# Attention scores from two fp32r parts instead of three bf16 parts, in a four-batch cross-attention block on one Trainium2 core

## What is computed

```python
B, LQ, LK, D, H, HD, INNER = 4, 256, 512, 256, 16, 16, 1024
# layer 0
q = layer_norm(x, ln1_w, ln1_b) @ q_w + q_b        # per head of 16
k = ctx @ k_w + k_b;  v = ctx @ v_w + v_b
scores = where(mask, q k^T / sqrt(16), lowest)
out = softmax(scores) v
hidden = out @ cproj_w + cproj_b + x
x = hidden + gelu(layer_norm(hidden, ln2_w, ln2_b) @ fc_w + fc_b) @ proj_w + proj_b
# layer 1, one head, on the same context
scores = (x w_q^T) (ctx w_k^T)^T / 16
x = x + alpha * (softmax(scores) (ctx w_v^T)) w_o^T
```

## Time and profile before

| | |
|---|---|
| Median of three runs | 315.48 us |
| Lowest, highest | 314.37, 318.81 us |
| Span of the profiled execution, first to last instruction | 310.4 us |
| Its own time | not given apart; the median is 5.1 us above the span |
| Busy: PE, weight loads, DVE, ACT, POOL | 87%, 63%, 67%, 61%, 38% |
| Mean granted TensorE clock | 0.960 |
| DMA | 21163 packets, 21.62 MB |

### The profile page before, as it was taken

One profiled execution on the slowest core, in us unless ns is written; L12 is line 12 of the kernel. 1 busy time (PEld: TensorE's weight loads), 2 busy tenths in 40 slices (PEclk: granted clock), 3 DMA queues, 4 the chain that ended last, 5 costly groups with the idle time before them and its releaser, 6 DMA issues.

```text
span 310.4 us, 5591 instructions
## 1 busy us (share of the span) xinstructions
PE 268.6 (87%) x2073; PEld 195.3 (63%) x2073; DVE 206.8 (67%) x367; ACT 187.8 (61%) x351; POOL 118.3 (38%) x174
## 2 busy tenths in 40 slices
PE   3974769998788999899979997999998989898995
PEld 2670236683266676665866766665966777677974
DVE  5774777729657859576569598657388655366854
ACT  1553367759464686967454887766466678426622
POOL 3574652523111369830012688430131256324100
PEclk9997599989797999999999999999999999999999
DMA  5597552522254002124112112121130000000001
GB/s 176 173 155 104 141 157 94 163 72 67 78 154 126 12 25 67 57 74 126 64 38 99 28 59 70 34 80 51 34 130 3 0 1 2 2 0 0 2 34 36
DMA packets 21163, 21.62 MB, mean 70 GB/s; under 512 B 4608, under 2 KB 17616, under 8 KB 21136
## 3 DMA queue, kind: packets, MB, share of 16 engines
q1 hardware_dynamic: 16880, 13.09, 14.8%
q0 software_dynamic: 1648, 3.87, 4.9%
q10 hardware_dynamic: 2608, 4.30, 4.6%
HBM read 10.50 MB, written 1.05 MB: 37 GB/s over the span
## 4 chain that ended last, share of the span: by engine, by line
PE 56%; ACT 13%; POOL 11%; DVE 9%; issue 5%; DMA 3%; ACTq 2%; POOLq 0%; DVEq 0%
PE work_ps L602 10%; PE om L679 8%; PE s L652 7%; PE work_ps L589 6%; PE s L669 6%; PE work_ps L606 5%; DVE neg_max L1442 4%; ACT q_stack L1100 3%; ACT probs L1109 2%; POOL y_l L1833 2%; PE s L602 2%; DMA q_stack<-qp 2%; POOL kf L1793 1%; ACT fx L1136 1%; POOL ft L1828 1%
## 5 line engine op out<-in xcount | busy, mean ns | idle before, releaser
L1442 DVE TENSOR_REDUCE neg_max<-s 128x1 f32<-128x512 f32 x128 | 83.5, 683 | 23.1 <-PE s L652 21.9
L1109 ACT ACTIVATE probs<-s 128x512 f32<-128x512 f32 x128 | 75.3, 601 | 32.4 <-PE s L669 31.8
L652 PE MATMUL s<-k_stack,q_stack 97*128 97x512 bf16 x128 | 49.8, 424 | 8.2 <-DMA q_stack<-qp 4.9
L669 PE MATMUL s<-q_stack,k_stack 109*128 109x256 bf16 x256 | 51.8, 286 | 2.0 <-ACT probs L1109 1.0
L679 PE MATMUL om<-probs,vals 128*17 128x256 f32 x512 | 34.5, 390 | 0.2 <-ACT probs L1109 0.2
L669 PEld LDWEIGHTS s<-q_stack,k_stack 109*128 109x128 bf16 x256 | 21.0, 102 | 19.0 <-ACT probs L1109 5.0
L652 PEld LDWEIGHTS s<-k_stack,q_stack 97*128 97x128 bf16 x128 | 13.0, 102 | 28.8 <-DVE neg_max L1442 14.3
L1763 POOL CAST max_cols<-neg_max 128x8 bf16<-128x8 f32 x16 | 6.1, 381 | 63.2 <-DVE neg_max L1442 63.2
L1100 ACT ACTIVATE q_stack<-om 13x1024 bf16<-13x1024 bf16 x16 | 16.3, 1017 | 9.1 <-PE om L659 8.8
L679 PEld LDWEIGHTS om<-probs,vals 128*17 128x17 f32 x512 | 12.0, 98 | 13.7 <-issue 6.2
L1123 ACT ACTIVATE y_h<-work_ps 128x512 fp32r<-128x512 f32 x12 | 7.2, 596 | 16.3 <-PE work_ps L606 14.5
(11 more groups left out here) (328 smaller groups left out, 724.5 us busy)
## 6 DMA issues: line engine op xcount, KB each, us to landing
k_stack<-kp SPq DMA_DIRECT2D x96, 64.0 KB
q_stack<-qp SPq DMA_DIRECT2D x81, 32.0 KB
cx<-in_ctx_dram SPq DMA_DIRECT2D x4, 512.0 KB, 4.7
pcx<-in_ctx_dram ACTq DMA_DIRECT2D x3, 512.0 KB, 3.6
xz<-in_x_dram SPq DMA_DIRECT2D x4, 256.0 KB, 2.7
raw_late<-in_L_xattn_fc_w_dram POOLq DMA_DIRECT2D x1, 1024.0 KB, 5.4
raw_late<-in_L_xattn_proj_w_dram POOLq DMA_DIRECT2D x1, 1024.0 KB, 6.7
h<-in_x_dram ACTq DMA_DIRECT2D x3, 256.0 KB, 2.6
```

The costliest lines, as they stand in the source:

```text
L652: pe.matmul(s1[:, s1_bank(b, SLOTS * g + s), :], q_stack[0:ROW_MAX, hd, chunk(t)], k_stack[0:ROW_MAX, hd, :], start=True, stop=True).then_ ...
L669: mm = pe.matmul(s2[:, s2_bank(b, SLOTS * g + s), i * LQ:(i + 1) * LQ], k_stack[:, hd, chunk(k)], q_stack[:, hd, :], start=True, stop=True)
L1109: act.activation(probs[:, g % 2, s // 2, k:k + 2, :], s2[:, s2_bank(b, SLOTS * g + s), :].rearrange("p (k n) -> p k n", k=2), ACT.Exp).the ...
L1442: dve.tensor_reduce(neg_max[:, g % 2, s % 2, s // 2:s // 2 + 1], s1[:, s1_bank(b, SLOTS * g + s), :], AX.X, ALU.max, negate=True).then_inc ...
```

## The change

Two fp32r parts take the place of three bf16 ones. There are three terms of 16 rows (high x high, high x low, low x high), 16 rows of ones against zeros, so that the mask row is at partition 64, and 8 rows for the maxima in two parts: 65 rows for the maxima tiles, 73 for the exp tiles, in fp32r of 4 bytes. The stacks hold three groups, which rotate; a group has seven transfers (three queries, mask row, three keys), and they wait until the group three before has been scored. All transfers of the start are SP's, and the loads of late weights move from POOL's queue to the end of SP's start.

The context lies transposed in DRAM as well (arranged on the host ahead of the launch), and so do the query and key weights with their columns in group order and all vectors in one array. ACT and DVE split the loaded context from SBUF; the eight transposes of PRE and of CT0/CT1 per batch are gone, with their uses of the work banks. CT0/CT1 remain as steps of ACT and DVE that read a second load, `pT_raw`. WA moves from the start to slot 12 of the first batch, into a work bank. Tables are laid anew; in `POST_FIRST` slots DVE does the work of batch b - 1 ahead of the projections.

```diff
-TERMS_Q = (0, 0, 1, 0, 1, 2)
-TERMS_K = (0, 1, 0, 2, 1, 0)
-ROW_MASK = len(TERMS_Q) * HD
+TERMS_Q = (0, 0, 1)
+TERMS_K = (0, 1, 0)
+ROW_MASK = P // 2
 ROW_MAX = ROW_MASK + 1
-ROWS = ROW_MAX + 3 * GH
+ROWS = ROW_MAX + 2 * GH
+STACK_GROUPS = 3
...
-PRE_AT = {7: 0, 8: 1, 9: 2, 10: 3, 14: 4, 19: 5}
+CT_AT = {7: 0, 8: 1}
+CT_LOW_AT = {8: 0, 9: 1}
+PRE_AT = {9: 0, 10: 1, 16: 2, 22: 3}
...
             def stack_group(b, g):
-                await_(sp, s2_full, NS * (b - 1) + SLOTS * (g + 1))
+                await_(sp, s2_full, SLOTS * (NG * b + g - STACK_GROUPS + 1))
                 stack_queries(b, g)
                 stack_keys(b, g)
...
-                if step in ("CT0", "CT1"):
-                    c = int(step[2])
-                    wait_context(pe, b)
-                    o = open_(W_CT + c)
-                    for k in range(TK):
-                        mm = pe.transpose(o[:, chunk(k)], pcx[:, k, chunk(c)], ident[:])
-                    fill(mm, W_CT + c)
-                elif step == "OT":
+                if step == "OT":
...
-                    await_(act, q_parts, b)
-                    if b == 0:
-                        act.wait_ge(pre_free, pre_use(b, U_K))
-                    for c in range(DC):
-                        act.activation(qf[:, c, :], pre_bank(b, n)[:, c * LQ:(c + 1) * LQ], ACT.Identity, bias=bq[:, c:c + 1])
                     for c in range(DC):
-                        a = act.activation(qp[:, 0, c, :], pre_bank(b, n)[:, c * LQ:(c + 1) * LQ], ACT.Identity, bias=bq[:, c:c + 1])
-                    a.then_inc(pre_free, 1)
+                        a = act.activation(qp[0][:, c, :], pre_bank(b, n)[:, c * LQ:(c + 1) * LQ], ACT.Identity, bias=bq[:, c:c + 1])
+                    a.then_inc(qh_done, 1)
...
+            def context_high(b, c):
+
+                act.wait_ge(cx_in, 16 * (b + 1))
+                await_(act, pre_full, PRE_USES * b)
+                act.activation(cT[0][:, c, :], cx[:, c, :], ACT.Copy).then_inc(ct_high, 1)
...
+            def context_low(b, c):
+
+                dve.wait_ge(ct_high, DC * b + c + 1)
+                dve.tensor_tensor(cT[1][:, c, :], cx[:, c, :], words(cT[0][:, c, :]), ALU.subtract).then_inc(ct_done, 1)
...
+                elif n == U_Q:
+
+                    dve.wait_ge(qh_done, b + 1)
+                    for c in range(DC):
+                        i = dve.scalar_tensor_tensor(qp[1][:, c, :], pre_bank(b, n)[:, c * LQ:(c + 1) * LQ], bq[:, c:c + 1],
+                                                     qp[0][:, c, :].bitcast(F32), ALU.add, ALU.subtract)
+                    i.then_inc(pre_free, 1)
...
-                pool.tensor_copy(part[0], neg).then_inc(max_step, 1)
-                pool.wait_ge(max_step, step + 1)
-                pool.tensor_tensor(max_rest[:], neg, part[0], ALU.subtract).then_inc(max_step, 1)
-                pool.wait_ge(max_step, step + 2)
-                pool.tensor_copy(part[1], max_rest[:]).then_inc(max_step, 1)
-                pool.wait_ge(max_step, step + 3)
-                pool.tensor_tensor(part[2], max_rest[:], part[1], ALU.subtract).then_inc(max_split, 1)
+                pool.tensor_copy(part[0], neg).then_inc(max_step, 1)
+                pool.wait_ge(max_step, NG * b + g + 1)
+                pool.tensor_tensor(part[1], neg, part[0].bitcast(F32), ALU.subtract).then_inc(max_split, 1)
```

506 lines of the change are left out of this document (217 added, 289 removed).

## The result

The changed kernel took 328.63 us (median of four runs, 323.89 to 330.79), the kernel before 317.01 beside it (four runs, 314.37 to 318.81). The ratio is 1.036, its 95% interval 1.030 to 1.042: slower by 11 us, where 14 us faster were forecast. The profiled execution of the changed kernel is one of its longer ones (330.79 us, span 329.1, clock 0.907; two others had spans of 322.1 and 324.7 at clock 0.921), so its middle batches are read beside those of the experiments.

What follows compares the result with a forecast made beforehand. It took a serial chain to bound the start, TensorE's stream and waits the middle batches. Terms -7.1 + 2.0 - 3.4 - 4.0 - 1.0 = -13.5 on 315.5 gave 302, set at 301 us (296 to 306; overall range 292 to 311).

Steps and rivals of the forecast that it cites:

- The waits that go: TensorE's waits for cT_l (-3.4 us) and POOL's split of the maxima (-4.0) shrink; less low clock, -1.0.
- one low stretch, 94.7 to 98.1 us: Clock at half behind a TensorE wait at slot 7; 1.7 us lost, -1.0 taken, bounds 0 and -1.7.
- The rows alone do not pay: TensorE's stream: additions of 7.3 us outweigh the 5.3 saved by 48 removed transposes, +2.0.
- The start: Before the first scores: shorter serial chain, first score at 19 to 22 us instead of 26.57; -7.1 us, bounds -4.5 and -8.5.
- TensorE's stream: Transposes removed, dearer score matmuls, row transposes and WA added: +2.0 us, bounds 0 and +3.5.
- what I counted at nothing: Added DVE operations and context and pT splits reading SBUF twice: zero, bounds -2 and +5 us.
- the split of the maxima: TensorE's waits for POOL outside the start, 7.9 us, halve: -4.0, bounds -2 and -7.
- (1): Group 3's stack transfers land late, ACT waits at slot 10: 0 to 2.5 us per batch, 310 us; with its like, chance 0.17.
- (3): Weight loads of fp32r score matmuls become exposed, up to 33 us: 334 us; with losses of like size, chance 0.09.
- (2): TensorE's waits go wholly and the clock stays full, 20.6 us less: 295 us, chance 0.22.

Runs made afterwards that it cites:

- e7: New kernel with score tiles over 97 and 105 rows, pcx and pT_raw loaded later, and late weights behind group 3's transfers: 316.2 us, ratio 1.005.
- e9: e7 with a new start: selector copied by ACT, three early SP transfers instead of POOL's four memsets: 311.1 us, ratio 0.991.
- e13: e7 with exp tiles over 128 rows, filled by the memsets and selector copy already there: 312.8 us, ratio 0.994.
- e11: New kernel with pcx and pT_raw loaded later and late weights behind group 3's transfers, rows left at 65 and 73: 321.0 us, ratio 1.025.
- e17: e13 with a new start: two POOL memsets and two transfers fill places 1 and 2, 32-row copy awaited before the keys: 311.5 us, ratio 0.993.
- e14: e9 with rows put back to 65 and 73: 318.4 us, ratio 1.015.
- e15: Kernel before, with only the maxima tiles reading 65 rows instead of 97: 317.8 us, ratio 1.014.
- e5: New kernel with ROW_MASK 96 instead of 64, so tiles read 97 and 105 rows: 322.8 us, ratio 1.026.
- e18: The same code as e9, measured again: 310.6 us, ratio 0.987.
- e3: New kernel with the selector copied by ACT and POOL's four memsets for places 1 and 2 replaced by transfers: 328.7 us, ratio 1.050.
- e4: New kernel with score matmuls reading only the upper 16 bits of each stack word, as bf16 over 65 and 73 rows: 321.1 us, ratio 1.023.
- e12: e7 with score matmuls reading only the upper 16 bits of each stack word, as bf16: 311.3 us, ratio 0.988.

## Why the prediction was wrong

**The step that failed** is the clock. In "The waits that go" I took one low stretch, 94.7 to 98.1 us, as a consequence of a wait and counted 1.0 us back; of the rows I wrote "The rows alone do not pay", and for the rest "no row shows 65 or 73 rows". I had no term for what 32 rows fewer do to the granted clock, nor for the 21 us at half that the kernel before has outside that one stretch. The new kernel has 61.4 us at half instead of 24.6 (two of its other runs had a mean clock of 0.921, which on a span of 322 is 2 x 0.079 x 322 = 51 us).

What it costs can be read from the table. The piece from exp 72 to 104 takes 65.0 us with none at half (e7, e9, e13), 66.3 with 3.4 (e11, e17) and 67.4 with 6.8 (the new kernel, e14). From exp 8 to 104, 184.7 us go with 10.2 at half (e17), 188.8 with 20.0 (e9), 193.5 with 33.0 (e14). That is about 0.4 us for each us at half; e15 against the kernel before has the same (4.5 for 10.6). The new kernel has 36.2 us more of it than the kernel before between these marks: 14 us by this estimate in the profiled execution, some 10 in the runs at 0.921.

Not all of that is the rows'. e15 shows that the rows do it with nothing else changed; e7 against e11 and e14 against e9 show it in the new kernel, at 5 to 7 us. Late transfers lower the clock as well: with both edits of e11, 29.0 us at half are left of 46.5. And e9, with rows, transfers and start mended, still has 20.0 there, 9.7 more than the kernel before, and a ratio below 1. How much each gives depends on what stands beside it: rows were 3.0 us alone (e5) and 6 with the transfers mended. In sum 14 of the 26 us between forecast and measurement are given back on the way to e9: 3 by the transfers, 6 by the rows, 4.4 by the start. The other 11 or 12 are gains that I had counted and that did not come.

**The start** (-7.1, first score at 19 to 22). What covers the links was wrong, and so was the last link. I counted DVE's own work and not what POOL does beside it. Three operations of DVE took 3.2 to 3.7 us; behind the first of them cT_l ended at 10.8 us (9.3 in e9), where I had 8.4. What came last was not the landing of the queries: TensorE's value projections, which I had ending near 19, ended at 25.3, behind wv_l and in part at half clock. The first score came at 25.31, 1.3 us earlier than before. With the memsets out of the way it came at 20.34 (e9; 21.95 in e18), and the first exp 6.7 us (5.1 in e18) before that of the kernel before. I looked for trouble with POOL only in subtractions of two SBUF tiles. Those took 0.68 us for cT_l (as costed) and 1.04 for pT_l:

```profile
L1419 DVE TENSOR_TENSOR pT_l<-pT_raw,pT_h 128x512 fp32r<-128x512 f32 x6 | 6.2, 1037 | 2.1 <-ACT pT_h L1117 2.0
L1366 DVE TENSOR_TENSOR cT_l<-cx,cT_h 128x512 fp32r<-128x512 f32 x8 | 5.4, 684 | 0.3 <-ACT cT_h L1082 0.3
```

The Trainium skill (SBUF — State Buffer, on SBUF's two separate sides) names a second case beside that of two SBUF inputs: a VectorE operation in a two-port mode and any GpSimd operation exclude each other for a whole instruction. The 3.59 us of a 128x2 TENSOR_SCALAR beside memsets, 0.17 without them (e3), agree with it; in which mode the operation ran the trace doesn't show.

**TensorE's stream** (+2.0). Score tiles are 0.24 and 0.12 apart as said; the type of the score tiles costs 4 to 5.5 us by e4 and e12, against 3.9 counted for them (2.6 + 1.3). A middle batch at full clock takes 65.0 us in e9 and 64.5 before, where the sum had it at about 62. So the 16 transposes a batch that went (48 x 0.11 in the sum) and the waits that went did no more than pay for what was added; no run takes the two apart. The sum itself had a slip: its bad ends add up to +1.0, not -4, once the +5 of what I counted at nothing is taken in, as its -2 was for the good ends. The measured time lies beyond either.

**The waits that go** (-3.4 and -4.0). The cT_l waits went, as forecast. For the split of the maxima 3.3 us came instead of 4, and of that little reached the end. POOL's own share is right, two operations less; behind it stands DVE. POOL of the new kernel, first split in the second middle batch:

```profile
207.55 1.28 POOL L1756 TENSOR_TENSOR h<-h,pb 128x512 f32<-128x512 f32 x1
210.65 0.59 POOL L1720 CAST max_cols<-neg_max 128x8 fp32r<-128x8 f32 x1 [1.82 <-DVE neg_max L1402]
211.32 0.21 POOL L1722 TENSOR_TENSOR max_cols<-neg_max,max_cols 128x8 fp32r<-128x8 f32 x1
211.58 0.44 PE L676 MATMUL om<-ident,max_cols 128*73 128x128 f32 x2 [0.93 <-POOL max_cols L1722]
```

POOL stood idle for 1.82 us and waited for DVE's last maximum. A faster POOL gives nothing there.

**The rivals.** (1), the late stack, had its mark: ACT waited for k_stack<-kp_l for 8.5 us in two. It was in a middle batch, where I had put it (5.3 us), and in the first batch as well, where I had not looked (3.2): I counted 4.5 us of SP per group and forgot the megabytes that this queue issues ahead of group 3. Priced by e11 it is 3 us, about as I had it (0 to 2.5 in each of three batches). (3), exposed weight loads, was the only rival on the right side (0.09, half of it slower by over 2%), and by e4 and e12 its mechanism is not what happened. The half sentence that a rate by rows used is part of it was the nearest I came. (2) did not come.

## What to carry to other kernels

A matmul that fills fewer rows of the array is not free even where its own time is the same: in this kernel the clock then stayed low longer, and more rows of zeros won time. Read the granted clock of each stretch first, and give it its own term in the sum for every change of rows, not only of waits. Before a copy or a small operation is counted as hidden, look at what is queued ahead of it on its queue and what POOL runs beside it.
